# A second buffer for the skip branch and one buffer less in the feed-forward part, with a new order of work on every engine

## What is computed

```python
def attn(u):                                  # u = layernorm(x)
    zxbcdt = u @ W_in.T                       # z0, x0, xBC, dt
    xBC = silu(causal_conv4(xBC))             # x, B, C
    h_t = exp(dt_t * A) * h_{t-1} + dt_t * x_t * B_t
    y_t = h_t . C_t + D * x_t
    y = layernorm(y) * ln_gamma + ln_beta
    y = sigmoid(y @ W_gate.T + b_gate) * y
    return concat([silu(z0) * x0, y]) @ W_out.T
def ffn(x):
    h = gelu(x @ absmean(W_fc).T)             # 256 -> 1024
    h = (h - mean) * rsqrt(var + eps) * ln_w + ln_b
    return h @ absmean(W_proj).T              # 1024 -> 256
x = x + attn(layernorm(x)); x = x + ffn(layernorm(x))
```

## Time and profile before

| | |
|---|---|
| median of 3 runs | 1179.52 us (1178.36 to 1180.4) |
| the profiled execution | 1178.07 us, of which its span is 1176.1 us |
| PE busy | 1109.2 us (94%) |
| DVE busy | 982.8 us (84%) |
| ACT busy | 953.7 us (81%), of it 119 table loads 152.7 us |
| POOL busy | 373.4 us (32%) |
| granted clock of TensorE | 0.99 of full |

### The profile page before, as it was taken

One profiled execution on the slowest core, in us unless ns is written; L12 is line 12 of the kernel. 1 busy time (PEld: TensorE's weight loads), 2 busy tenths in 40 slices (PEclk: granted clock), 3 DMA queues, 4 the chain that ended last, 5 costly groups with the idle time before them and its releaser, 6 DMA issues. The chain is left out here.

```text
span 1176.1 us, 23319 instructions
## 1 busy us (share of the span) xinstructions
PE 1109.2 (94%) x8534; PEld 721.4 (61%) x8534; DVE 982.8 (84%) x1958; ACT 953.7 (81%) x1675; POOL 373.4 (32%) x500
## 2 busy tenths in 40 slices
PE   3879999999999999999999999999999899999995
PEld 1455757576665756666575675756757475667663
DVE  5999997999789987888988887898978888686654
ACT  4867778898798997889887979968979977867855
POOL 1121233234323414242243333323323332332422
PEclk9989999999999999999999999999999999999998
DMA  6411222252424343242442424443353251343455
GB/s 189 150 47 21 63 55 55 47 118 37 81 65 91 74 75 79 54 109 46 81 83 44 96 44 90 80 63 89 60 109 46 45 92 37 67 70 71 76 123 109
DMA packets 238977, 89.14 MB, mean 76 GB/s; under 512 B 207760, under 2 KB 235152, under 8 KB 238864
## 3 DMA queue, kind: packets, MB, share of 16 engines
q1 hardware_dynamic: 238864, 87.67, 36.1%
HBM read 24.32 MB, written 8.39 MB: 28 GB/s over the span
## 5 line engine op out<-in xcount | busy, mean ns | idle before, releaser
L359 PE MATMUL bank<-xnT,win 128*128 128x512 f16 (+1 forms) x1248 | 295.9, 384 | 25.0 <-DMA xnT<-hb 20.4
L359 PEld LDWEIGHTS bank<-xnT,win 128*128 128x128 f16 (+1 forms) x1248 | 120.9, 101 | 158.0 <-issue 27.9
L945 DVE SCALAR_TENSOR_TENSOR cv<-bank,cws,cv 128x510 f32<-128x510 f32 (+5 forms) x240 | 177.6, 744 | 14.5 <-ACT tail L676 4.4
L359 PE MATMUL bank<-yhl,wg 128*128 128x512 f16 x768 | 171.9, 379 | 1.9 <-DVE yhl L1092 1.2
L180 ACT ACT_TABLE_LOAD x119 | 152.7, 1283 | 2.8 <-PEq L1386 0.7
L1212 POOL TENSOR_TENSOR cat<-sz,cat 128x512 f16<-128x512 f32 x64 | 81.5, 1277 | 221.6 <-ACT cat L782 221.6
L587 PE MATMUL bank<-wpj,hT 128*128 128x256 f16 x1024 | 123.1, 276 | 8.8 <-DMA hT<-hb 8.6
L1208 POOL TENSOR_TENSOR caty<-tg,caty 128x512 f16<-128x512 f32 x64 | 81.3, 1277 | 157.7 <-ACT caty L770 157.5
L359 PEld LDWEIGHTS bank<-yhl,wg 128*128 128x128 f16 x768 | 73.9, 98 | 91.0 <-issue 3.1
L575 PE MATMUL bank<-wfc,x3T 128*128 128x512 f16 x512 | 121.8, 379 | 3.1 <-DMA x3T<-hb 2.5
L587 PEld LDWEIGHTS bank<-wpj,hT 128*128 128x128 f16 x1024 | 100.1, 99 | 30.1 <-issue 10.8
(11 more groups left out here) (145 smaller groups left out, 2091.7 us busy)
## 6 DMA issues: line engine op xcount, KB each, us to landing
x<-in_x SPq DMA_DIRECT2D x32, 512.0 KB, 4.2
out_y<-x SPq DMA_DIRECT2D x15, 512.0 KB, 3.2
crep<-cv SPq DMA_DIRECT2D x128, 32.0 KB, 2.0
hT<-hb SPq DMA_TRANSPOSE x128, 3.2
caty<-in_wg SPq DMA_DIRECT2D x1, 1024.0 KB, 8.1
x<-in_wout SPq DMA_DIRECT2D x1, 1024.0 KB, 6.6
hT<-in_wfc SPq DMA_DIRECT2D x1, 1024.0 KB, 9.2
hn<-in_wpj SPq DMA_DIRECT2D x1, 1024.0 KB, 12.5
```

Of the source, the lines that this page charges most:

```text
L359: m = eng.matmul(b, lhs(p, k), rhs(q, k), start=(n == 0), stop=(n == len(seq) - 1))
L945: op = eng.scalar_tensor_tensor(cs[0:w, j, 3 - k:T], b[0:w, 0:T - 3 + k], cws[0:w, j, k:k + 1], cs[0:w, j, 3 - k:T], ALU.mult, ALU.add)
```

## The change

Three things change beside the tables and the shift of line numbers by one or two that they bring.

1. `cat` gets a second buffer, by the block's parity. ACT `l` of block i now waits for PE `o` of block i-2. In block 1 it also waits until the preparation of W_proj is done, whose staging area now lies in the second `cat` (it lay in `hn`).
2. `hn` is dropped: DVE `i` writes its result over the Gelu's result in `h`. So DVE `i` waits for ACT `q` (the squares, the last reader of Gelu's result) where it waited for ACT `m` (the mean), and ACT `g` of a chunk waits until both halves of the chunk two before are made.
3. The five tables list the same steps in a new order, with new banks.

```diff
-        cat = sb("cat", [P, 2, 4, T], f16)
+        cat = sb("cat", [P, 2, 2, 4, T], f16)
...
-        hnb = sb("hn", [P, 2, 1024])
+        hnb = h
...
-        wps = hnb[:, :, :].rearrange("p n f -> p (n f)")
+        wps = cat[:, 1].rearrange("p a f t -> p (a f t)").bitcast(f32)
...
             def half_cat(i, j):
                 act.wait_ge(sx, 4 * i + j + 1)
-                act.wait_ge(out_mm, 4 * i)
-                eng.activation(cat[:, 0, j, :], sz[:, j % 2, :], ACT.Copy).then_inc(cat_hi, 1)
+                act.wait_ge(out_mm, 4 * (i - 1))
+                if i == 1:
+                    act.wait_ge(gam_v, 3)
+                eng.activation(cat[:, i % 2, 0, j, :], sz[:, j % 2, :], ACT.Copy).then_inc(cat_hi, 1)
...
             def gelu_h(i, n):
...
-                act.wait_ge(hn, at - 1)
                 if half == 0:
-                    act.wait_ge(h_sq, at - 1)
+                    act.wait_ge(hn_hi, at - 1)
+                    act.wait_ge(hn_lo, at - 1)
...
             def centre_h(i, c):
                 at = 4 * i + c
                 dve.wait_ge(ld_lnw, 16)
-                dve.wait_ge(h_mu, at + 1)
-                dve.wait_ge(hn_hi, at - 1)
-                dve.wait_ge(hn_lo, at - 1)
+                dve.wait_ge(h_sq, at + 1)
...
 PE_ORDER = (
-    "c00 c01 u02 c03 z04 c05 c06 z07 z00 v02 v01 c13 u14 m05 c17 c12 x06 x03 v04 b07 c15 x06 x00 g03 z02 e05 s06 "
+    "c00 c01 u02 c03 z04 v05 c06 c07 m00 z02 v01 b04 c13 c12 z05 s00 u16 x07 x05 c13 x01 e00 x07 v05 c12 g00 O03 "
```

More of the change, by code:

```diff
@@ L557, in lhs @@
                 def lhs(p, k):
-                    t = cat[:, p, k, :] if k < 4 else caty[:, p, k - 4, :]
+                    t = cat[:, i % 2, p, k, :] if k < 4 else caty[:, p, k - 4, :]
                     return t[:, chunk(c)]
@@ L1211, in rest_cat @@
                 pool.wait_ge(cat_hi, 4 * i + j + 1)
-                eng.tensor_tensor(cat[:, 1, j, :], sz[:, j % 2, :], cat[:, 0, j, :], ALU.subtract).then_inc(cat_lo, 1)
+                eng.tensor_tensor(cat[:, i % 2, 1, j, :], sz[:, j % 2, :], cat[:, i % 2, 0, j, :], ALU.subtract).then_inc(cat_lo, 1)
             def norm_x2(i, n):
```

## The result

| | before | after |
|---|---|---|
| median | 1179.3 us (7 runs, 1177.08 to 1180.4) | 1184.46 us (7 runs, 1181.78 to 1184.78) |
| the profiled execution, its span | 1178.07, 1176.1 us | 1183.04, 1181.0 us |

The changed kernel is slower: ratio 1.004, 95% interval 1.0029 to 1.0052, 5 us. Forecast were 1175.3 us and a gain; the time lies inside the range of 1164 to 1186.

A forecast was written before the change was run, and what follows sets the result against it. PE was taken to bound the middle, DVE the head, and a chain through ACT, DVE and transposing DMAs the tail. 1178.07 - 4.0 - 2.2 + 2.0 = 1173.9; the median lying 1.45 higher, 1175.3 us; range 1164 to 1186.

The forecast's parts named there:

- the middle: Between the first gate and the last 66 us: added table loads make PE wait, partly offset by skip-branch work; +2 us.
- the tail: Last 66 us: PE work moved behind the last `o`, a POOL wait gone, shared buffer slower; -2.2 us.
- the head: Up to PE's first gate: fewer DVE rows ahead of `yhl` let the gate start earlier; -4.0 us.
- Doubling this in the dense stretches: Blocks 3 to 5 and 7 to 9: PE's idle 2.5 and 2.0 us there doubles under added loads; some 4 us.
- the filling: Middle: skip branch, run ahead through the second `cat`, gives PE work while it would wait; takes back half of 4 us.
- ACT becomes the bound: Blocks 3 to 5 and 7 to 9: table loads delay the ACT step that frees PE's bank; 1183, chance 0.23.
- The rival on the gate of block 2: PE waits 4 us for DVE at that gate, so the head's gain is lost; 1179, chance 0.18.
- -3.5 - 0.6 + 1.9: Tail: PE work moved behind the last `o`, block f's first `o` no longer waiting for POOL, shared buffer's later halves.
- The part moved behind: Tail: two `f` and one `p` of block e now follow the last `o` steps, where PE idles; gain 3.5 us.
- just fits: Tail: block e's last chunk needs about 5.6 us on ACT in a gap of 5.5 us.

The follow-up runs named there:

- light POOL: From block 2 on, GpSimd's three wide kinds of work done on an eighth of the columns, in either kernel: before 1161.28 us, after 1159.61 us.

## Why the prediction was wrong

The time is 9.2 us over the forecast: the middle 6.6 over its term, the tail 2.7, the head 0.2 under.

**Head: right.** Forecast -4.0 with the first gate near 97; measured -4.2, gate at 97.21.

**Middle: wrong, and the step that failed** is "Doubling this in the dense stretches and nothing elsewhere gives some 4 us, of which I let the filling take half back: +2 us". It was +8.6. The load on ACT was forecast well. The dense stretches of after, from the end of block 2's scaling to that of block 5, and from 7 to 9:

```profile
204.30:428.60 224.30, 218.80 (x1686) 142.36 (x1685) 193.12 (x381) 201.42 (x338) 76.43 (x99) 0.98 0.34 69
552.60:702.40 149.80, 146.86 (x1170) 95.63 (x1168) 132.17 (x274) 132.77 (x230) 45.54 (x64) 1.00 0.33 70
```

ACT 201.4 us of 224.3 and 132.8 of 149.8 (forecast 201 of 224 and 133 of 144). What was wrong was to turn this share into a price by doubling an idle time of 2.5 and 2.0 us, since those idle times are the small visible part: light POOL took 18 us out of before, and PE's idle time in the middle only fell from 19.1 to 9.0 us. What the runs showed in its place is longer stops of PE at a few places (six over 1.5 us, two before) and the clock behind them: matmuls at 1.2 GHz make 7.3 of the 8.6 us. In the first dense stretch the granted clock is 0.98, where it was 1.00 in the earlier trace rows. The sum had no term for the clock. And it had none for VectorE meeting GpSimd, though it was in the trace of before (46 stretched instructions, 41 us) and the order of both engines was changed. How much of the 8.6 us goes back to meetings and how much to loads stays open. The rival "ACT becomes the bound" gave 1183, which is the size that came; that is luck in part, as its mechanism is at most half of it. PE didn't wait for ACT in those stretches by several us: single waits of up to 2.7 us, for ACT and for DVE in turn, in all of the middle. The rival on the gate of block 2 has the right size and the wrong place: that gate still has 3.3 us of the lead, the next one none, and what PE waits for at 228.00 is the meeting. Whether more cover would have hidden it wasn't tried.

**The second buffer** wasn't tried alone. With loads and POOL's work out of the way the new order with it is 4.3 us ahead, which is no more than the head; no trace shows that it shortens the middle, for which I had allowed 2 us.

**Tail: the size was off.** Forecast -2.2 = -3.5 - 0.6 + 1.9, measured +0.5. The part moved behind is as forecast; from the last `o` to the end it takes 4.0 us longer, not 1.9. Timelines of ACT, PE and DVE at the end, after; the answer to the earlier trace rows:

```profile
1142.91 1.06 ACT L653 ACTIVATE hb<-x 128x1024 f16<-128x1024 f32 x1 [3.35 <-DVE x L1112]
...
1148.67 1.06 ACT L821 ACTIVATE hb<-h 128x1024 f16<-128x1024 f32 x1 [1.77 <-DVE h L1125]
...
1154.74 1.06 ACT L821 ACTIVATE hb<-h 128x1024 f16<-128x1024 f32 x1
...
1163.69 1.06 ACT L821 ACTIVATE hb<-h 128x1024 f16<-128x1024 f32 x1 [2.34 <-DMA hT<-hb]
...
1169.04 1.06 ACT L821 ACTIVATE hb<-h 128x1024 f16<-128x1024 f32 x1 [1.35 <-DVE h L1125]
```

```profile
1149.09 3.61 PE L575 MATMUL bank<-wfc,x3T 128*128 128x512 f16 x16 [1.45 <-DMA x3T<-hb]
...
1174.73 3.51 PE L587 MATMUL bank<-wpj,hT 128*128 128x256 f16 x16 [3.48 <-DMA hT<-hb]
```

```profile
1167.72 1.28 DVE L1125 SCALAR_TENSOR_TENSOR h<-h,hmu,lnwb 128x1024 f32<-128x1024 f32 x1 [1.21 <-ACT hsq L812]
```

From the half of `x2` to that of the first chunk 11.83 us (10.07 before, 11.2 forecast), as the last chunk of block e, which "just fits", is 1.77 us late for DVE. From the third chunk's half to the fourth's 5.35 us (4.44 before, 5.2 forecast). Between them -0.3. From the last half to the end 11.96 us, where it was 10.36: 1.6 us that I had no term for. They are the clock again: PE's last step, 16 matmuls, takes 3.51 us, and took 1.91 before. The stretches of the last `p` step, before and after:

```profile
1171.00:1176.20 5.20, 1.91 (x16) 1.49 (x16) 1.81 (x5) 0.00 (x0) 0.86 (x2) 1.00 0.55 182
```

```profile
1174.50:1181.00 6.50, 3.51 (x16) 2.25 (x16) 0.48 (x1) 0.00 (x0) 0.00 (x0) 0.74 0.41 135
```

After the longer idle time ahead (3.48 us) the granted clock of the last stretch is 0.74, most of the step at the level of 1.2 GHz. The length of the stop alone doesn't decide it: at 1157.74 of before the same step took 1.91 us behind a stop of 3.02. Sum: 1.8 + 0.9 - 0.3 + 1.6 = 4.0.

## What to carry to other kernels

Before an order is changed, look in the trace for instructions that take longer than others of their form, and for what runs beside them; if both engines' tables change, where they meet changes too, and a sum of moved work doesn't see it. When two edits each take the whole of a loss away, they act in part on the same time: price them together, by an edit with neither. Where PE is the bound, list its stops of over a microsecond and read the granted clock behind them before asking which engine is too full: here the time at the lower clock grew by more than the stops did. And a wait made shorter by cutting the instruction in two is paid by whoever waits for the whole.

## What the runs showed of the hardware

- VectorE instructions with two operands in SBUF (47 of 49), and `TENSOR_SCALAR` and `CAST` with one operand of four elements a lane or more (11 of 11), ended behind the wide GpSimd instruction within which they started; one-element ones didn't (0 of 13). GpSimd's wide work as a whole cost 18 of 1179 us in a kernel with PE 94% busy, most of it not visible as PE's idle time; how much of this is exclusion isn't shown.
- A VectorE instruction of 32 elements a lane took 1.07 to 1.25 us beside whole GpSimd instructions of 1.16 us, 0.64 to 0.65 us beside halves, and 0.18 to 0.19 us alone.
- TensorE's clock fell to 1.2 GHz at or some us behind stops of PE of 1.2 to 2.7 us in a kernel with PE 98% busy around them (granted clock 0.62 to 0.76 over the stretches shown), but not behind every one: the stop of 1.68 us at 761.2 of before has no fall behind it.
- PE's last 16 matmuls of 256 columns took 3.51 us at a granted clock of 0.74 behind an idle time of 3.48 us, and 1.91 us at 1.00 behind one of 1.18 us.
- A DMA costs its issuing engine too: SyncE was held 1.3 us by a transposing one and 6 us by eight small ones (32 KB each).
